# Moving the preparation of the deformable weights ahead of the second group's stem in a one-core vision-tower kernel

## The reference

```python
h = conv2d(x, stem_w, stem_b, 4)                 # 96 channels, 24 x 24
h = leaky_relu(batchnorm(h, bn1_g, bn1_b, bn1_m, bn1_v))
offset = conv2d(h, off_w, off_b, 4)              # 2 x 16 taps for each of 6 x 6 tokens
h = deform_conv(h, offset, dcn_w, dcn_b)         # 16 bilinear samples of h a token, then 96*16 -> 192
h = leaky_relu(batchnorm(h, bn2_g, bn2_b, bn2_m, bn2_v))
...
h = h + attn(layernorm(h)); h = h + ffn(layernorm(h))
```

## Time and profile before

| what | us |
|---|---|
| median of three executions | 564.36 (562.98 to 566.38) |
| profiled execution | 568.5 |
| its span | 566.7 |
| PE busy | 469.8 (83%) |
| DVE busy | 307.4 (54%) |
| ACT busy | 224.9 (40%) |
| POOL busy | 156.5 (28%) |

### The profile page before, as it was taken

How to read it: one execution, slowest core, us unless ns; L and a number is a source line. 1 busy time by engine, 2 the same in 40 slices (tenths; PEclk the granted TensorE clock), 3 DMA queues, 4 the chain that set the end, 5 groups by cost and what they waited for, 6 DMA issues and landing times.

```text
span 566.7 us, 7771 instructions
## 1 busy us (share of the span) xinstructions
PE 469.8 (83%) x2637; PEld 348.5 (61%) x2637; DVE 307.4 (54%) x1178; ACT 224.9 (40%) x527; POOL 156.5 (28%) x161
## 2 busy tenths in 40 slices
PE   3987456548983799989988899899888998998797
PEld 2464245426672588746776788467766876776575
DVE  3063048615645758185469972755598748373212
ACT  0621863202252354162543742625436422631321
POOL 3003747200471472000760740006608400000000
PEclk9977857776995569999999999999989999998799
DMA  4629525349972152007750640067504300000000
GB/s 103 144 53 244 161 74 153 91 108 269 262 202 56 33 161 63 0 1 178 206 147 1 186 116 1 1 162 206 159 4 132 108 2 0 1 1 16 0 1 16
DMA packets 59046, 54.17 MB, mean 96 GB/s; under 512 B 44354, under 2 KB 51167, under 8 KB 59007
## 3 DMA queue, kind: packets, MB, share of 16 engines
q1 hardware_dynamic: 49360, 25.32, 18.0%
q0 software_dynamic: 9216, 28.32, 17.6%
q10 hardware_dynamic: 431, 0.03, 0.0%
HBM read 38.60 MB, written 15.06 MB: 95 GB/s over the span
## 4 chain that ended last, share of the span: by engine, by line
PE 62%; DVE 17%; ACT 8%; issue 5%; POOL 3%; SPq 2%; DMA 2%; ACTq 1%; DVEq 0%; POOLq 0%
PE bank L729 11%; PE bank L742 11%; PE bank L556 6%; PE bank L467 6%; PE bank L482 4%; PE bank L653 3%; PE bank L672 3%; PE bank L489 3%; POOL ring L428 3%; ACT h L862 2%; PE bank L615 2%; PE bank L657 2%; SPq L371 2%; PE bank L696 2%; DVE o L1217 2%
## 5 line engine op out<-in xcount | busy, mean ns | idle before, releaser
L428 POOL DMA_INDIRECT ring<-cells,cell x144 | 145.3, 1009 | 258.6 <-DVE corner L1116 116.2
L729 PE MATMUL bank<-xfT,w_up 96*128 96x288 f32 x288 | 84.6, 444 | 2.5 <-ACT hid L993 2.5
L742 PE MATMUL bank<-w_down,hid 128*128 128x192 f32 (+1 forms) x432 | 79.1, 339 | 2.4 <-ACT hid L993 2.4
L742 PEld LDWEIGHTS bank<-w_down,hid 128*128 128x128 f32 (+1 forms) x432 | 62.9, 167 | 15.3 <-ACT hid L993 4.2
L556 PE MATMUL bank<-w_dcn,shared 128*128 128x192 f32 (+1 forms) x288 | 62.1, 365 | 7.3 <-ACT shared L890 7.3
L729 PEld LDWEIGHTS bank<-xfT,w_up 96*128 96x128 f32 x288 | 56.5, 206 | 18.7 <-ACT hid L993 3.9
L993 ACT ACTIVATE hid<-bank,b_up 128x288 f32<-128x288 f32 x72 | 35.4, 500 | 69.5 <-PE bank L729 69.4
L1131 DVE SCALAR_TENSOR_TENSOR bank<-ring,corner,bank 128x96 f32<-128x96 f32 x224 | 52.9, 312 | 16.0 <-ACT bank L881 15.9
L556 PEld LDWEIGHTS bank<-w_dcn,shared 128*128 128x128 f32 (+1 forms) x288 | 47.0, 181 | 21.0 <-ACT shared L890 9.4
L467 PE MATMUL bank<-xt,w_stem 96*96 96x384 f32 x96 | 43.5, 588 | 3.4 <-ACT h L862 3.3
L862 ACT ACTIVATE h<-bank,bn_bias,bn_scale 96x384 f32<-96x384 f32 x48 | 31.3, 667 | 32.3 <-PE bank L467 32.3
(11 more groups left out here) (153 smaller groups left out, 633.0 us busy)
## 6 DMA issues: line engine op xcount, KB each, us to landing
cells<-ring SPq DMA_DIRECT2D x16, 864.0 KB, 9.5
xs<-in_x_dram SPq DMA_DIRECT2D x32, 108.0 KB
ring<-cells,cell POOLq DMA_INDIRECT x144, 3.1
w_up<-in_L_ffn_W_dram SPq DMA_DIRECT2D x2, 864.0 KB, 12.4
w_down<-in_L_ffn_W_dram SPq DMA_DIRECT2D x3, 576.0 KB, 15.6
hid<-in_L_tok_dcn_w_dram SPq DMA_DIRECT2D x1, 1152.0 KB, 8.8
out_dram<-y SPq DMA_DIRECT2D x8, 96.0 KB, 2.0
w_qk<-in_L_attn_W_qkv_dram SPq DMA_DIRECT2D x24, 24.0 KB, 1.8
```

What stands on the lines that cost most here:

```text
L428: pool.indirect_dma_start(ring[:, ring_slot(k), j, :], None, table[0:HALF_CELLS, :] if k < EARLY else table, bass.IndirectOffsetOnAxis(ap= ...
L729: mm = pe.matmul(ps[5 + n % 2][:, 0:TOK], w_up[:, kt, e, 128 * f:128 * f + 128], xfT[:, kt, :], start=(kt == 0), stop=(kt == 1))
L742: mm = pe.matmul(down_out(e, t), hid[:, e % 2, f, t0:t0 + n], w_down[:, e, f, :], start=(f == 0), stop=(f == FCH - 1))
```

## The change

On ACT, `scale_dcn` takes its half m as an argument and is called inside `stem_ht(0)`: four of its instructions stand ahead of the copies of rows of half 0, and four ahead of those of half 1. The six copies to `w_dcn` and that of the bias row stand right behind `stem_ht(0)`, ahead of `stem_bn(1, 0)`. On PE, `dcn_weights`, `dcn_bias` and the wait for their copies stand behind `offsets_by_token(0)`, ahead of the stem of group 1, and the first of them waits for six copies of `xt` in place of twelve. Nothing is added or left out; DVE, POOL and SP have the same lists as before.

```diff
@@ PE, dcn_weights @@
                 if u == 0:
                     pe.wait_ge(dcn_scaled, 8)
-                    pe.wait_ge(xt_evac, 12)
+                    pe.wait_ge(xt_evac, 6)
                     pe.wait_ge(nat_evac, 3)
@@ PE, order @@
             offsets_by_token(0)
 
-            pe.wait_ge(nat_evac, 2)
-            for s in range(2):
-                stem_x(1, s)
-                stem_products(1, s)
             for u in range(6):
                 dcn_weights(u)
             dcn_bias()
             pe.wait_ge(w_dcn_evac, 7)
+            for s in range(2):
+                stem_x(1, s)
+                stem_products(1, s)
@@ ACT, stem_ht @@
                 for s in range(2):
+                    if g == 0:
+                        scale_dcn(s)
                     for j in range(0, 6, 2):
@@ ACT, scale_dcn @@
-            def scale_dcn():
+            def scale_dcn(m):
                 act.wait_ge(ld_dcn, 16)
-                for m in range(2):
-                    for q in range(QUADS):
...
+                for q in range(QUADS):
...
@@ ACT, order @@
             stem_bn(0, 1)
             stem_ht(0)
             act.wait_ge(zeroed, 5)
+            for u in range(6):
+                dcn_weights(u)
+            act.wait_ge(w_dcn_mm, 7)
+            act.activation(bias2, ps[5][0:1, 0:C2], ACT.Copy).then_inc(w_dcn_evac, 1)
             act.wait_ge(feat_ready, 1)
             stem_bn(1, 0)
             stem_xt(1)
             stem_bn(1, 1)
-            scale_dcn()
-            for u in range(6):
-                dcn_weights(u)
-            act.wait_ge(w_dcn_mm, 7)
-            act.activation(bias2, ps[5][0:1, 0:C2], ACT.Copy).then_inc(w_dcn_evac, 1)
             combine_start(0)
```

More of the change, by code:

```diff
@@ L891, in samp_copy @@
                                ACT.Copy).then_inc(samp_evac, 1)
-            def scale_dcn():
+            def scale_dcn(m):
                 act.wait_ge(ld_dcn, 16)
-                for m in range(2):
-                    for q in range(QUADS):
-                        src = dcn_nat[:, m, :].rearrange("o (i c j q) -> o q i j c", i=CHUNKS, c=32, j=BATCH)[:, q, :, :, :]
-                        act.activation(dcn_perm[:, m, q, :].rearrange("o (i j c) -> o i j c", i=CHUNKS, j=BATCH), src, ACT.Copy,
-                                       scale=bn_scale[:, 1 + m:2 + m]).then_inc(dcn_scaled, 1)
+                for q in range(QUADS):
+                    src = dcn_nat[:, m, :].rearrange("o (i c j q) -> o q i j c", i=CHUNKS, c=32, j=BATCH)[:, q, :, :, :]
+                    act.activation(dcn_perm[:, m, q, :].rearrange("o (i j c) -> o i j c", i=CHUNKS, j=BATCH), src, ACT.Copy,
+                                   scale=bn_scale[:, 1 + m:2 + m]).then_inc(dcn_scaled, 1)
             def dcn_weights(u):
```

## The result

| what | before | changed |
|---|---|---|
| median of four executions | 563.96 us (562.98 to 566.38) | 558.94 us (556.59 to 559.43) |
| ratio | | 0.9896 [0.9854, 0.9939] |
| profiled execution | 568.5 | 556.59 |
| its span | 566.7 | 554.7 |
| granted clock of PE, mean | 0.901 | 0.907 |

The changed kernel is 5.0 us faster by the medians and 1.0% by the ratio, whose interval comes to 3.4 to 8.2 us. The forecast was 2.5 us, 561.9.

What follows compares the result with a forecast made beforehand. POOL's gathers and SP's loads were taken to bound the kernel until 127.64. The last gather gains 7.6 us less 5.1 for a held gather, 2.5 us: 564.4 - 2.5 = 561.9 us, range 558.0 to 563.6.

Steps and rivals of the forecast that it cites:

- The bound: Group 0 until 127.64: POOL's gathers, then SP's attention loads, set the end; PE idles 7.33 us ahead of the last load.
- Everything behind 127.64 moves by the same amount.: From PE's start behind the attention's weights on, all work shifts by the last gather's gain, 2.5 us.
- rival 2: PE's clock behind the attention's weights, 133 to 140: at 0.50 time is 564.2, at 1.00 560.6; chance 0.13, half each.
- The scalings: ACT, group 0: first four cost nothing with 0.4 us to spare; second four delay the first gather by 0.2 us.
- The stem of group 1: PE and ACT: later by 1.4 us at most, or about 1 us earlier if the clock stays at 1.00.
- POOL's wait: Ahead of group 0's twenty-first gather: 6.30 us waiting for DVE, to vanish with some 5 us of cover.
- The hold: Group 0: DVE's 24 sums with two tensors in SBUF hold one POOL gather, costing 5.1 us of 7.6 gained.
- rival 1: Group 0 gathers slip through DVE's run: 560.6 us for one, 556.8 if none is held; chance 0.14.
- The base: Profiled execution against median, 4.1 us apart: no cause found in the moved work, so the gain is carried over whole.
- The bound of 0.5%: Whole kernel: about 0.5% (2.8 us) can't be told from no change; chances 0.44 faster, 0.52 within, 0.04 slower.

Runs made afterwards that it cites:

- psum_after_b: Changed kernel with group 0's first two running sums (batches 0 and 1) in PSUM; 558.6 us, ratio 0.9895 to the kernel before.
- late_half: Changed kernel with the second four scalings behind all copies of rows, on a slower chip; 639.68 against 646.1 us for the kernel before, ratio 0.9857.
- only_scale_b: Kernel before with only the eight scalings moved, turns and copies of the weights left behind the stem of group 1; 562.92 us, ratio 0.9932.

## Why the prediction was right, and where it was off

- **The bound.** Right. The chain runs from the first corners through DVE and POOL to SP's loads in both kernels, and the stretch from last gather to L482 hardly moved (25.04, 23.84, and 24.66 in the second trace of the change). The gain up to there is 4.6 us by the traces (4.81 less 0.22), and the median gained 5.0. The agreement is a loose one: the interval of the gain is 3.4 to 8.2 us, and `psum_after_b` took another 1.8 us and more off the gathers without a better time.
- **"Everything behind 127.64 moves by the same amount."** Not so in the traces: from L482 on the changed kernel took 4.44 us less, 3.3 of them in group 1 by PE's clock. The prediction gave the clock a price and a chance (its rival 2) only for the stretch right behind the weights. There both traces have 0.50 to about 7 us behind the start of L482, and the difference came some 65 us further on. What part of it belongs to the change is open, so a part of the measured 5.0 us may be the clock's.
- **The scalings.** Right. The first four cost nothing, with 0.1 us to spare in this trace rather than 0.4 (in `late_half` ACT waited 0.44 us for PE behind them); the second four cost 0.22 us where 0.2 was said, which is also the size of the scatter of that stretch.
- **The stem of group 1.** Right, in the better of its two cases. PE's clock no longer falls ahead of it. Busy time by stretch in the kernel before, with the granted clock third from the end:

```profile
52.00:54.00 2.00, 2.00 (x5) 0.82 (x4) 0.14 (x1) 0.67 (x1) 1.44 (x2) 0.50 1.02 253
```

  The same stretch in the changed kernel, where PE had turned weights in place of waiting for DVE, is at the higher level:

```profile
52.00:54.00 2.00, 1.79 (x6) 0.63 (x5) 0.00 (x0) 1.52 (x3) 1.70 (x2) 1.00 0.91 255
```

  DVE's run began at 63.30, or 65.1 with the 1.77 us of the early stem put back; the prediction had 65.6 to 68.2, so it came half a us ahead of the earliest. The 24 turns took 2.51 us at 1.00, where about half of 4.1 was said.
- **POOL's wait.** Right: gone, and the trace of `only_scale_b` shows that the scalings alone are enough for that where PE isn't late.
- **The hold.** Right in mechanism, and it is the term that was mis-sized. The prediction took 5.1 us (4.7 to 5.6; its own terms give up to 5.9 for a gather held in flight); the traces show 3.07 and 1.7 us, and 3.8 with only the scalings moved. Its step "either the gather in flight is held, or it slips out and the next is held" allowed one gather to get through, and rival 1 gave it one in five. The count over six traces is 17 of 35, and of the eight gathers in flight none was held. In the whole change two and three gathers got through a run of 5.59 us before one was held. The forecast and its rival 1 were the same mechanism, and what happened lies between them. With the measured holds in place of 5.1 the sum is lower by 2.0 and 3.4 us, 559.9 and 558.5, and 558.94 was measured. That it comes so near is in part luck, since the clock's share isn't in this sum.
- **The base.** The profiled execution lay 4.1 us over its median, and the prediction found nothing for that in the moved work. The trace has 34.1 us at the lower clock in group 1, where the changed kernel has 27.3. Matmuls that take 3.71 us at one level and 2.11 at the other would make about 3 us of this. It is not in the moved work itself, but whether moving it shortens that stretch isn't known.
- **The bound of 0.5%.** The forecast lay just within it, the result beyond. The chance of 0.44 for faster came from a gain that hangs on one term, whose size changes from trace to trace. That the time lies inside the stated range (558.0 to 563.6) owes something to the width given to the median's scatter: the forecast itself is 3.0 us off.

## What to carry to other kernels

When a change starts an engine earlier, look for what it will then run beside, not only for what it no longer runs behind. Here 24 sums of DVE moved from a time at which POOL stood still into the middle of its gathers, and gave back 1.7 to 3.8 of 7.6 us. Look too whether the held instruction is on the chain: the gather of 191.42 was held for 2.5 us and cost nothing. Work moved off the path is worth only what the next wait leaves uncovered: by its trace, a part of this move removed POOL's wait just as well. And where a collision has few cases in one trace, count its outcomes before giving it one price, or keep both outcomes with like chances.

## What the runs showed of the hardware

- A gather issued by POOL that meets sums of DVE with two tensors in SBUF either passes in 0.94 to 1.11 us or is held until 0.4 to 0.8 us behind the end of the whole unbroken run (12 or 24 instructions), in 17 and 18 of 35 cases. With one tensor in PSUM none of the 36 gathers was above 1.12 us. The Trainium skill (SBUF — State Buffer, Who interferes with whom) has the second one block fully; the held cases agree, those that pass don't.
- What decides between the two I can't say. In group 2 the same picture, one that passes and one that takes 1.87 us, came back within 0.02 us in four of the traces, so it isn't chance alone; the start against the run (0.14 us when it passed in group 2 and 0.14 when it was held in group 3 of the changed kernel) doesn't decide it either.
- In the first stem ACT got a product every 1.28 us at first and every 0.85 later, and the change of pace falls where the clock's record begins, at 1.00: at 25.96 in the kernel before (products at 24.46, 25.74, 26.58) and at 21.34 in the changed one (19.59, 20.86, and two every 1.71 us from 23.32 on). What the views print as 1.00 ahead of that is no record. In group 1 of the kernel before the same products come every 1.28 us at 0.50 and every 0.85 at 1.00. So the first products very likely ran at the lower level, and the late stem of that trace is a clock that rose 4.6 us later. ACT's rows in the first stem and in group 1 of the kernel before:

```profile
19.75 0.67 ACT L862 ACTIVATE h<-bank,bn_bias,bn_scale 96x384 f32<-96x384 f32 x1 [0.61 <-PE bank L467]
21.03 0.67 ACT L862 ACTIVATE h<-bank,bn_bias,bn_scale 96x384 f32<-96x384 f32 x1 [0.61 <-PE bank L467]
...
28.29 0.67 ACT L862 ACTIVATE h<-bank,bn_bias,bn_scale 96x384 f32<-96x384 f32 x1 [0.17 <-PE bank L467]
...
54.15 0.67 ACT L862 ACTIVATE h<-bank,bn_bias,bn_scale 96x384 f32<-96x384 f32 x1 [0.53 <-PE bank L467]
55.43 0.67 ACT L862 ACTIVATE h<-bank,bn_bias,bn_scale 96x384 f32<-96x384 f32 x1 [0.61 <-PE bank L467]
```

- The same kernel took 564 and 566 us on two occasions and 646 and 650 us on two other chips, with products of the stem up to 4.2 us apart and pauses of DVE between instructions without a wait that the trace could name.
